# Expert blocks from two tables: the first 13 between the last dispatch steps, the other 26 from the final counts

## What is computed

```python
probs = softmax(xt @ Wg)                      # 8 experts
topk_p, topk_i = top_k(probs, 2)              # weights divided by their sum
h = gelu(xt @ W1[e] + b1[e])                  # F0: 512 hidden; F1: silu(x@gate) * (x@up), 256
out = sum over the two e of p_e * (h @ W2[e] + b2[e])
```

## Time and profile before

| | us |
|---|---|
| Median of 3 runs | 1561.71 |
| The runs | 1553.89, 1561.71, 1562.01 |
| Span of the profiled execution | 1552.4 |
| Its busy time: PE, PEld, DVE, ACT, POOL | 1214.8, 936.1, 1011.3, 902.7, 771.3 |

### The profile page before, as it was taken

One profiled execution on the slowest core, in us unless ns is written; L12 is line 12 of the kernel. 1 busy time (PEld: TensorE's weight loads), 2 busy tenths in 40 slices (PEclk: granted clock), 3 DMA queues, 4 the chain that ended last, 5 costly groups with the idle time before them and its releaser, 6 DMA issues. The chain is left out here.

```text
span 1552.4 us, 31341 instructions
## 1 busy us (share of the span) xinstructions
PE 1214.8 (78%) x11210; PEld 936.1 (60%) x11218; DVE 1011.3 (65%) x2376; ACT 902.7 (58%) x1718; POOL 771.3 (50%) x590
## 2 busy tenths in 40 slices
PE   6898989898768887675599938998699886538882
PEld 2666766676564665454499935666356664428772
DVE  5999999999997786555111117886379675433334
ACT  3988898889744886442355527776366453213333
POOL 1999999998954123444355531110113243346552
PEclk8999999999999998766699979999799787659996
DMA  5241222122000311111688732000200001047665
GB/s 191 84 143 55 111 84 84 56 111 84 28 1 8 56 40 31 51 34 55 198 246 257 231 79 55 15 16 16 75 2 25 24 26 35 29 146 208 204 204 174
DMA packets 98028, 138.51 MB, mean 89 GB/s; under 512 B 13965, under 2 KB 77402, under 8 KB 93684
## 3 DMA queue, kind: packets, MB, share of 16 engines
q1 hardware_dynamic: 85764, 117.08, 25.3%
q0 software_dynamic: 9088, 17.07, 3.2%
q10 hardware_dynamic: 3024, 2.36, 0.5%
HBM read 105.91 MB, written 28.19 MB: 86 GB/s over the span
## 5 line engine op out<-in xcount | busy, mean ns | idle before, releaser
L353 POOL TENSOR_TENSOR M_dbx<-M_u,M_b_sb 128x1024 f32<-128x1024 f32 x127 | 296.8, 2364 | 33.2 <-DVE M_e L440 15.5
L454 DVE TENSOR_TENSOR_SCAN M_h<-M_pA,M_dbx 128x512 f32<-128x512 f32 x256 | 298.2, 1207 | 6.5 <-ACT M_pA L612 6.2
L612 ACT ACTIVATE M_pA<-M_dt,M_a_neg 128x504 f32<-128x504 f32 x256 | 175.0, 684 | 21.7 <-DVE M_h L454 17.4
L2159 POOL DMA_INDIRECT F_slots<-F_line,F_pos x128 | 127.1, 993 | 54.4 <-issue 37.9
L2532 PE MATMUL X_bank<-F_xT,F_wbuf 128*128 128x256 f32 x624 | 152.4, 388 | 0.0
L1864 PE MATMUL X_bank<-L_ident,X_s_sb 128*128 128x128 f32 x512 | 94.6, 312 | 69.7 <-ACT X_pt_sb L1727 63.0
L622 ACT ACTIVATE M_hc<-M_pT,M_cT 128x256 f32<-128x256 f32 x256 | 119.8, 469 | 42.9 <-PE M_pT L759 41.5
L1727 ACT ACTIVATE X_pt_sb<-X_bank 128x512 f32<-128x512 f32 x128 | 76.3, 596 | 105.7 <-PE X_bank L1864 105.4
L1552 DVE TENSOR_REDUCE X_smax<-X_bank 128x8 f32<-128x512 f32 x128 | 82.3, 685 | 82.7 <-PE X_bank L1855 80.9
L775 PE MATMUL M_pY<-M_ident,M_hc 128*128 128x128 f32 x1024 | 135.1, 275 | 0.4
L775 PEld LDWEIGHTS M_pY<-M_ident,M_hc 128*128 128x128 f32 x1024 | 125.0, 192 | 0.3
(11 more groups left out here) (339 smaller groups left out, 2810.1 us busy)
## 6 DMA issues: line engine op xcount, KB each, us to landing
M_b_sb<-M_rows_bc SPq DMA_DIRECT2D x32, 1024.0 KB, 4.7
F_wbuf<-in_F_wcat SPq DMA_DIRECT2D x39, 578.0 KB
F_wbuf<-in_F_wcat SPq DMA_DIRECT2D x39, 450.0 KB
X_s_sb<-F_slots SPq DMA_DIRECT2D x39, 132.0 KB
F_xblk<-F_slots SPq DMA_DIRECT2D x39, 132.0 KB
F_line<-F_line SPq DMA_DIRECT2D x16, 256.0 KB
S_ya<-F_answers SPq DMA_DIRECT2D x16, 256.0 KB, 5.7
F_slots<-F_pad ACTq DMA_DIRECT2D x16, 132.0 KB
```

The source lines that it names most:

```text
L353: pool.tensor_tensor(dbx[:, k % DBXS, :, :], u[:, g % 2, :, :], bc(b_sb[:, n, :], 1, 2), ALU.mult).then_inc(dbx_ready, 1)
L454: v.tensor_tensor_scan(h[:, k % STATES, half, :], pA[:, (2 * k + half) % DECAYS, :, :].rearrange("p b t -> p (b t)"), dbx[:, k % DBXS, hal ...
L612: act.activation(pA[:, (2 * k + half) % DECAYS, :, 1:SEQ], dt[:, g % 2, half, :].rearrange("p (b t) -> p b t", t=SEQ)[:, :, 1:SEQ], ACT.Ex ...
L2159: pool.indirect_dma_start(slots, bass.IndirectOffsetOnAxis(pos[:, g, k, t:t + 1], 0), line[:, g % RING, k, t, :], None, bounds_check=E * C ...
```

## The change

Blocks are taken from two tables. After group 4 (`FIRST_GROUPS` = 5), 5120 of the 8192 rows are counted. Since at most 8 x 255 rows can stand in blocks not yet full, at least 13 blocks are full (`FIRST_BLOCKS`). `vector_first_table`, 15 DVE instructions at step 32, lists these 13. The second table lists the remaining 26 after the final counts. In detail:

- Blocks 0 to 10 run at steps 35 to 45 on TensorE, ACT and DVE, behind the step's own work; the first two turns and the first hidden layer stand at the end of step 34 (`LEAD`). The rest follows after step 45.
- SP loads the first weights behind the first table, then does group 6's twin and store, waits for the scatters of groups 0 to 4, and loads blocks 0 to 12. Group 7's twin and store come after block 6. The 8 pads move from ACT to SP, 4 after block 9 and 4 after block 10. `rows_written` is waited for at block 13.
- POOL: group 7's rstd moves from between the first and second pair of group 6's scatters to before them; answer 0 follows at step 37, answers 1 and 2 at step 41, the others after group 7's scatters.
- Ranks of groups 6 and 7 move one step earlier (36 and 40), ahead of the residual on DVE; counts are summed twice.
- Turns and outputs have one PSUM bank each (4 and 5), since 6 and 7 are still in use.
- The weights' exponents stand after block 14 on ACT, the weights after block 16 on DVE, F0's transposes after block 18; x is read back beside blocks 14 to 29.

```diff
+FIRST_GROUPS = 5
+FIRST_BLOCKS = -(-(2 * GROUP * FIRST_GROUPS - EXPERTS * (BLOCK - 1)) // BLOCK)
+REST_BLOCKS = BLOCKS - FIRST_BLOCKS
+FULL = FIRST_GROUPS * GROUP // BLOCK
+RANKED_EARLY = {STEPS + 4: GROUPS - 2, STEPS + 8: GROUPS - 1}
...
+    def sync_pads(sp, lo, hi):
+        sp.wait_ge(tail_ready, 1)
+        for e in range(lo, hi):
+            t = sp.value_load(tail[0:1, e:e + 1], min_val=0, max_val=E * CAP - BLOCK)
+            sp.dma_start(slots[bass.ds(t, BLOCK), :].rearrange("(p s) c -> p s c", s=SUBS),
+                         pad[:, :, :]).then_inc(pads_in, 16)
...
+    def vector_first_table(v, link):
+        N = FIRST_BLOCKS
+        turn = turns[:, 0:N]
+        link(v.tensor_tensor(first_over[:, :, :], bc(first_count[:, :], 2, FULL), bc(plan[0:1, 1:FULL + 1], 1, E), ALU.is_ge))
+        link(v.tensor_reduce(left[:, :], first_over[:, :, :], AX.X, ALU.add))
+        add_up(v, link, first_upto, left[:, :], first_incl[:, 1:E + 1])
+        link(v.tensor_scalar(first_incl[:, 1:E + 1], first_incl[:, 1:E + 1], float(N), None, ALU.min))
+        link(v.tensor_tensor(taken[:, 0:E], first_incl[:, 1:E + 1], first_incl[:, 0:E], ALU.subtract))
...
-        if place == "first" and s == 1 and in_range(c - 3):
-            ranks(pe, c - 3)
-            if c - 3 == GROUPS - 1:
-                counts(pe)
+        if place == "first":
+            g = RANKED_EARLY.get(i, c - 3 if s == 1 and i < STEPS + PER else -1)
+            if in_range(g):
+                ranks(pe, g)
+                if g in (FIRST_GROUPS - 1, GROUPS - 1):
+                    counts(pe, g)
...
-    H0, Y0, X0 = 0, 4, 6
+    H0, X0, Y0 = 0, 4, 5
...
+    def sync_first_blocks(sp, rows_of, store):
+        sp.wait_ge(d.table_ready, 1)
+        sync_weights(sp, 0)
+        sync_weights(sp, 1)
+        rows_of(sp, GROUPS - 2, store)
+        d.first_rows_written(sp)
+        if homes is not None:
+            sp.wait_ge(att.pt_psum, 2 * STEPS)
+        for j in range(FIRST_BLOCKS):
+            if j >= 2:
+                sync_weights(sp, j)
+            sync_block(sp, j)
+            if j == 6:
+                rows_of(sp, GROUPS - 1, store)
+            if j in (9, 10):
+                d.sync_pads(sp, (j - 9) * E // 2, (j - 8) * E // 2)
...
     def turn_block(pe, j):
         pe.wait_ge(xblk_in[j % XBUFS], 16 * (j // XBUFS + 1))
-        reach(pe, bT_ready, j - 1)
+        reach(pe, bT_ready, j)
...
-        reach(pe, y_done, j - 1)
+        if j == 0:
+            pe.wait_ge(att.o_used, 2 * GROUPS)
+        reach(pe, y_done, j)
...
+    LEAD = STEPS + 2
+    WEIGHTS_AT = 16
+    ANSWERED = {STEPS + 5: (0,), STEPS + 9: (1, 2)}
+    ANSWERED_EARLY = 3
...
-                if g == GROUPS - 2 and n == 0:
+                if g == GROUPS - 3 and n == PER - 1:
                     d.pool_normal(pool, GROUPS - 1)
-            f.pool_answers(pool)
+                for j in ANSWERED.get(i, ()):
+                    f.pool_answers(pool, j)
+            for j in range(ANSWERED_EARLY, BLOCKS):
+                f.pool_answers(pool, j)
...
+                if i == STEPS:
+                    d.vector_first_table(v, link)
+                if i in RANKED_EARLY:
+                    d.place(v, link, RANKED_EARLY[i])
+                if i == STEPS + 8:
+                    d.vector_tail(v, link)
+                if i == STEPS + 9:
+                    d.vector_table(v, link)
...
+                if i > LEAD:
+                    f.vector_block(v, i - LEAD - 1)
...
+                if i == LEAD:
+                    f.tensor_lead(pe)
+                if i > LEAD:
+                    f.tensor_block(pe, i - LEAD - 1)
```

More of the change, by code:

```diff
@@ L2083, in dispatch_stage, with sync_rows, first_rows_written @@
     st.sync_loads = sync_loads
[L2085 to L2090, removed]
-    st.sync_rows = sync_rows
[L2094 to L2101, removed]
+    def sync_rows(sp, g, store):
+        sp.wait_ge(xn_ready, g + 1)
+        reach(sp, scattered[g % RING], 16 * 2 * TILES * (g // RING))
+        sp.dma_start(line[:, g % RING, 1, :, 0:D], line[:, g % RING, 0, :, 0:D]).then_inc(twin_in[g % RING], 16)
+        store(sp, g)
+    st.sync_rows = sync_rows
+    def sync_pads(sp, lo, hi):
[4 more added lines that the diff above has]
+                         pad[:, :, :]).then_inc(pads_in, 16)
+    st.sync_pads = sync_pads
+    def first_rows_written(sp):
+        for r in range(RING):
+            sp.wait_ge(scattered[r], 16 * 2 * TILES * ((FIRST_GROUPS - r + RING - 1) // RING))
+    st.first_rows_written = first_rows_written
     def rows_written(sp):
@@ L2371, in ring_uses @@
         return (BLOCKS - i + n - 1) // n
-    EARLY_WEIGHTS = 2
-    def sync_blocks(sp, beside):
[L2376 to L2406, removed]
@@ L2407, in sync_blocks @@
+    st.sync_first_blocks = sync_first_blocks
+    def sync_blocks(sp, beside):
+        sp.wait_ge(d.table_ready, 2)
+        for j in range(FIRST_BLOCKS, BLOCKS):
+            sync_weights(sp, j)
+            if j == FIRST_BLOCKS:
+                d.rows_written(sp)
+            sync_block(sp, j)
             if beside is not None:
@@ L2423, in expert_stage, with pool_answers @@
     st.sync_answers = sync_answers
[L2425 to L2432, removed]
+    def pool_answers(pool, j):
+        pool.wait_ge(y_done, j + 1)
+        for s in range(SUBS):
+            pool.indirect_dma_start(
+                answers, bass.IndirectOffsetOnAxis(xblk[:, j % XBUFS, s, D:D + 1].bitcast(I32), 0),
+                yblk[:, j % XBUFS, s, :], None, bounds_check=2 * TOKENS - 1,
+                oob_is_err=False).then_inc(y_out[j % XBUFS], 16)
     st.pool_answers = pool_answers
@@ L2450, in answer, with vector_block @@
         v.tensor_tensor(yblk[:, j % XBUFS, :, :],
-                        bank[:, Y0 + j % 2, 0:BLOCK].rearrange("p (s d) -> p s d", d=D),
+                        bank[:, Y0, 0:BLOCK].rearrange("p (s d) -> p s d", d=D),
                         bc(wbuf[:, j % WBUFS, W1 + W2 + MM:WCAT], 1, SUBS), ALU.add).then_inc(y_done, 1)
[L2454 to L2460, removed]
+    def vector_block(v, j):
+        if gated:
+            gate_up(v, j)
+            if j >= 1:
+                answer(v, j - 1)
+            if j == BLOCKS - 1:
                 answer(v, j)
-        if gated:
-            answer(v, BLOCKS - 1)
-    st.vector_blocks = vector_blocks
+        else:
+            answer(v, j)
+    st.vector_block = vector_block
     def vector_sum(v, link, g, weight):
@@ L2514, in expert_stage, with scalar_block @@
-    st.scalar_blocks = scalar_blocks
+    st.scalar_lead = scalar_lead
+    def scalar_block(act, j):
+        if gated:
+            act.wait_ge(h_psum, 2 * j + 1)
+            reach(act, gated_done, j - 1)
+        else:
+            reach(act, y_psum, j - 1)
+        for c in range(HC):
+            if not gated and c % 2 == 0:
+                act.wait_ge(h_psum, 2 * j + c // 2 + 1)
+            ins = act.activation((sg if gated else hT)[:, j % 2, c, :],
+                                 bank[:, H0 + 2 * (j % 2) + c // 2, c % 2 * BLOCK:(c % 2 + 1) * BLOCK], func,
+                                 bias=wbuf[:, j % WBUFS, W1 + W2 + c:W1 + W2 + c + 1])
+            if c % 2 == 1:
+                ins.then_inc(act_done, 1)
+        if j + 2 < BLOCKS:
+            copy_bT(act, j + 2)
@@ L2767, in _ @@
                 a.tensor_step(pe, i, d.tensor_others)
-            if guarded:
-                pe.wait_ge(d.weight_ready, 1)
-                for k in range(2):
-                    ins = pe.transpose(bank[0:LANES, 5, k * P:(k + 1) * P], d.weight[:, :, k], ident[:, :])
-                ins.then_inc(weight_psum, 1)
-                pe.wait_ge(weight_turned, 2)
-            f.tensor_blocks(pe)
+                if i == LEAD:
+                    f.tensor_lead(pe)
+                if i > LEAD:
+                    f.tensor_block(pe, i - LEAD - 1)
+            for j in range(LAST - LEAD - 1, BLOCKS):
+                f.tensor_block(pe, j)
+                if j == WEIGHTS_AT + 2 and guarded:
+                    pe.wait_ge(d.weight_ready, 1)
+                    for k in range(2):
+                        ins = pe.transpose(bank[0:LANES, 6, k * P:(k + 1) * P], d.weight[:, :, k], ident[:, :])
+                    ins.then_inc(weight_psum, 1)
     return f.answers
```

181 lines of the change are left out of this document (110 added, 71 removed).

## The result

Measured beside each other, the kernel before took 1556.88 us and the changed one **1569.73 us** (medians of 19 runs each, 1553.36 to 1567.41 and 1562.61 to 1579.71). The ratio is 1.0079, 95% interval 1.0059 to 1.0098: slower by 0.8%, where 1530 us, 2% faster, was forecast. The profiled execution spans 1574.3 us, against 1552.4 us.

A forecast was written before the change was run, and what follows sets the result against it. Bound by the dispatch tail ahead of each expert stage, up to some 36 us per layer. Block 11 earlier by 18.5 + 16 us, less 2.5 us for ACT's tables, gives 32 us: 1561.7 to 1530 us, range 1500 to 1554 us.

The forecast's parts named there:

- the working: Dispatch to first blocks: block 0 turns at 721.2 and 1352 us, block 11 at about 777 and 1408 us.
- a sign of being wrong: GpSimd idle between group 7's rstd and answer 3, where 24 instructions, 30.7 us, were expected without a gap.
- the wait that the text named: SP's wait for answer 3, said to cover the pads in F0; in F1 they may cost 0 to 3 us.
- rival D: Single banks make each of 78 blocks pay 1.2 us: 94 us slower against 32 gained, 1624 us; chance 0.07.
- the clock at 1.00 from the first blocks on: Sign of being right: TensorE's clock level stays at 1.00, the upper level of 2.4 GHz, once first blocks run.
- the step that set rival B aside: Argument on ACT's seven waits, 6.8 us in the mean, for sixteen groups: only groups 6 and 7 stand on this chain.
- rival B: Stickier pipeline: one 10 us stall per layer on the chain leaves 12 of 32 us gain, 1550 us; chance 0.12.
- The sum of the forecast: Block 11 earlier by 18.5 us in F0 and 16 us in F1, less 2.5 us for ACT's tables: 32 us.
- head start: How much earlier block 0 turns in each layer: 36.2 us in F0 and 35.9 us in F1.
- the term for the old block 11: Block 11's turn in F1 of the kernel before, from first blocks and mean pitch 3.46 us: 1423.8 us.
- the step said 1 us a stage: Exponent between blocks 14 and 15: two table loads, 2.6 us more ACT work, about 1 us reaching TensorE per stage.
- the 1.5 us for the pads: Pads moved to SP may cost 0 to 3 us in F1, where block 9's rows go out late; 1.5 taken.

The follow-up runs named there:

- first occasion: First measurement of the changed kernel beside the kernel before, chip not recorded: 1569.73 us against 1556.88 us, ratio 1.0079.
- after_again: The changed kernel, unchanged, measured again beside the kernel before on chip 11: 1437.01 us against 1454.65 us, ratio 0.9891.
- tick_after: The changed kernel with a 1x1 memset, waited for, after every two indirect DMAs on GpSimd, on chip 5: 1456.66 us, 1.0025 of the kernel before.

## Why the prediction was wrong, and where it was right

**Right.** On the first occasion block 0 turned at 721.7 us against 721.2, and rstd of group 7 ended at 741.44 + 1.04 = 742.48 us against 741.3 (the 729.8 us that stands beside it there is an end too). From block 0's turn to that end `after_again` has 709.19 - 689.9 = 19.3 us, forecast 20.1. The rest holds where no signal is held: block 11 follows block 0 there by 746.2 - 689.9 = 56.3 us in F0 and 57.7 us in F1; the working gave 55.8 and 56. GpSimd has no gap from answer 0 to answer 3, and block 11 waits for that answer, as claimed; on the first occasion GpSimd stood 11.87 us in that stretch, which the prediction had named as a sign of being wrong. TensorE's pitch after block 13 hardly changed (3.01 us in F1, 2.94 before). Pads on SP: covered, and by the wait that the text named. Single banks: nothing, by two runs; rival D falls. Not right on either occasion: the clock at 1.00 from the first blocks on. It was granted at 0.82 and 0.84 in the 10 us stretches from 730 and 740 us of `after_again`, where TensorE worked 5.95 and 8.30 us of 10.

**Wrong: the step that set rival B aside.** It took the seven "remote" waits of the earlier trace rows, up to 12.3 us, as something that only a group's transposes meet, priced at one 10 us stall per layer, and gave it 0.12, because "only those of groups 6 and 7 stand on this chain". The sum of the forecast itself has no term for it. The trace after shows an answer's signal held, a turn's, a hidden layer's and the logits', as well as a group's transposes. The change put the first blocks of each layer into the stretch where GpSimd scatters, and made its rows longer: 14 indirect DMAs where before mostly 6 to 8, once 10, came between pauses. It also hung more on each signal: the choice of group 7 is behind an answer on VectorE, and GpSimd's last scatters behind the choice. In place of 10 us per layer TensorE stood 13.68 + 13.31 = 27.0 us in F0 and 8.68 + 10.83 = 19.5 us in F1 in those waits, and ran slower behind them. The hidden layer after the first, and the stretches after both:

```profile
764.80 3.62 PE L2602 MATMUL X_bank<-F_xT,F_wbuf 128*128 128x256 f32 x8
```

```profile
764.00:768.00 4.00, 3.68 (x10) 3.06 (x11) 2.58 (x15) 1.22 (x3) 0.00 (x0) 0.50 0.56 182
793.00:797.00 4.00, 3.50 (x16) 3.53 (x17) 0.35 (x1) 1.81 (x5) 1.94 (x2) 0.50 0.36 125
```

The hidden layer takes 3.62 us where the earlier trace rows has 1.89 us: after standing 13 us TensorE was granted 0.50 in both places (1.2 GHz). Block 0 to block 11 took 802.0 - 721.7 = 80.3 us and 1441.7 - 1362.2 = 79.5 us, 24 us per layer more than worked out. With head starts of 35.7 us in F0 and, less the 7.2 us that F0 ends later, 32.9 us in F1, and 38.1 and 32.1 us for the same blocks before, that is 80.3 - 35.7 - 38.1 = 6.5 us and 79.5 - 32.9 - 32.1 = 14.5 us lost. The sum, 21.0 us, is nearly the difference of the spans, 21.9 us. That the late signals cause the loss is supported by the three chips without them on which both kernels ran, where the sign turns; it was not shown by removing them on the first occasion, and why they are late stays open.

**Wrong in size, where no signal is held.** The span fell by 20.6 us there, not 32. In F0 block 11 gains 761.3 - 746.2 = 15.1 us, not 18.5: the head start is 722.9 - 689.9 = 33.0 us, not 36.2, since the old dispatch tail is itself shorter without held signals (from group 6's rstd to block 0 42.0 us, where it was 46.6). In F1 it gains 8.5 us of its own (1339.7 - 1315.9 = 23.8, less 15.3 from F0), not 16. Most of that, 5.0 us, lies in the term for the old block 11: it was put at 1387.9 + 35.9 = 1423.8 us by a mean pitch of 3.46 us. The trace before has its turn at 1420.00 us, 3.8 us earlier, since the stage's first blocks are quicker than its mean. Without held signals it comes 30.9 us after block 0, another 1.2 us less, and the mean pitch is 2.93 us:

```profile
1420.00 0.38 PE L2520 MATMUL X_bank<-L_ident,F_xblk 128*128 128x128 f32 x2
```

Then 3.4 us are given back behind block 11 in F1; part of it is the exponent's tables:

```profile
1332.72 1.28 ACT L2326 ACT_TABLE_LOAD   x1
1334.01 0.23 ACT L2326 ACTIVATE F_e<-F_max 128x32 f32<-128x32 f32 x1
1334.15 0.40 ACT L2328 ACTIVATE F_ex<-F_lgs 128x256 f32<-128x256 f32 x1
1334.57 1.28 ACT L2576 ACT_TABLE_LOAD   x1
1335.86 0.84 ACT L2576 ACTIVATE F_sg<-X_bank,F_wbuf 128x256 f32<-128x256 f32 x2
```

```profile
1338.09 1.13 PE L2616 MATMUL X_bank<-F_wbuf,F_hT 128*128 128x128 f32 x8 [1.24 <-DVE F_yblk L2518]
```

ScalarE is taken for 1335.86 - 1332.72 = 3.14 us, and TensorE waits 1.24 us; the step said 1 us a stage, while the sum took 2.5 us for two, and did not name the 1.5 us for the pads. In F0 the pitch across it stays 3.75 us. Of the Trainium skill (ScalarE: Activation LUTs, What ACT_TABLE_LOAD costs) the 1.28 us of the load stands here, but its drain of some 1.38 us does not show: each load starts within 0.02 us of the end of the activation ahead of it, and the next activation 0.01 us after the load ends.

## What to carry to other kernels

When a wait in a profile names no releaser, compare it with the end of the work that should have released it. If that ended long before, do not take the wait for a property of the one instruction that shows it: here other signals of the same engine were late too. Price a change by how many of them it brings onto its path, and have a second chip's profile beside it before taking a pitch from one. Read the start of one given block from its row, not from a mean pitch. Count what a queue does during a wait: work that looks misplaced there (the pads) may be the best-placed work of all.

## What was unexpected of the hardware

- On the first occasion signals of TensorE came up to 14.7 us after the instruction that gives them, most of them released 1 to 2.5 us after a row of indirect DMAs of GpSimd ended: 87 us before, 138 us after, overlaps counted once. Signals of VectorE and ScalarE in the same profiles were at most 12 ns late. The changed kernel on chips 11, 12 and 4, the kernel before on chip 11 and variants of both on chip 5 had none over 1 us. The kernel before took 7% longer on the occasion that had them (1556.9 against 1454.7 us).
- The same change was 0.8% slower on that occasion and 0.9 to 1.1% faster on the three chips without them.
- With a 1x1 memset that is waited for between them, two indirect DMAs of GpSimd stand 0.88 us apart instead of 0.30 us; 142 such memsets made the changed kernel 15 to 19 us slower within a series. The rows of `tick_after`:

```profile
721.14 0.97 POOL L2188 DMA_INDIRECT F_slots<-F_line,F_pos  x1 [0.30 <-issue]
722.10 0.09 POOL L2041 MEMSET F_rest<- 1x1 f32 x1
722.99 0.97 POOL L2188 DMA_INDIRECT F_slots<-F_line,F_pos  x1 [0.80 <-POOL F_rest L2041]
```
